# Where TensorE's operands start in SBUF, modulo 256 bytes, and when the loop registers are set

## What is computed

```python
h = layernorm(x) * (1 + ca) + sa
xn = rms_scale * h / (norm(h) + EPS) * split_scale
K = sigmoid(xn @ W_K);  u, g_in, g_out = split(xn @ W_ugg, 3)     # 256 -> 512, 256 -> 3*512
u = u * sigmoid(g_in) * (1 - K)
y = scan(K shifted by one token, u) * sigmoid(g_out) @ W_out + h  # 512 -> 256
x = x + ga * y
h = layernorm(x) * (1 + cb) + sb
for e in range(8):                                               # the two best experts of a token count
    out += (gelu(h @ W1[e] + b1[e]) @ W2[e] + b2[e]) * weight[:, e]
x = x + gb * out
```

## Time and profile before

| | |
|---|---|
| median of three runs | 726.5 us |
| the profiled execution: time, span | 730.45 us, 728.5 us |
| PE busy, weight loads busy | 684.8 us, 625.1 us |
| DVE, ACT, POOL busy | 505.1, 417.0, 399.3 us |
| granted clock of TensorE, mean | 0.984 |
| matmuls L1107 and L1123 (experts), L998 (mixing) | 1536 and 1632, 768 |

### The profile page before, as it was taken

The page is one execution under the profiler, slowest core; times in us unless marked ns, Lnnn a source line. Parts: engine busy times, 40 slices in busy tenths (PEclk is TensorE's granted clock), DMA queues, the critical chain, the costliest instruction groups (busy, mean ns, idle before and its releaser), DMA issues.

```text
span 728.5 us, 16045 instructions
## 1 busy us (share of the span) xinstructions
PE 684.8 (94%) x4798; PEld 625.1 (86%) x4798; DVE 505.1 (69%) x1751; ACT 417.0 (57%) x1068; POOL 399.3 (55%) x318
## 2 busy tenths in 40 slices
PE   5799999999999998998989899999999999999992
PEld 2578878788888887898879899999999999999992
DVE  5869789998988796575754556558775575576451
ACT  4555655556565553664455656647666566566460
POOL 2165536796767567256653437337656356374443
PEclk9899999999999999899999999999999999999997
DMA  8370011302202323245544454567664655544433
GB/s 299 114 242 30 29 59 54 109 30 89 75 16 90 144 75 111 31 117 149 103 82 65 80 119 69 118 143 177 134 124 74 161 99 125 133 70 69 68 74 43
DMA packets 50603, 72.77 MB, mean 100 GB/s; under 512 B 5968, under 2 KB 42396, under 8 KB 50528
## 3 DMA queue, kind: packets, MB, share of 16 engines
q0 software_dynamic: 16480, 27.28, 21.4%
q1 hardware_dynamic: 34048, 44.60, 19.8%
HBM read 48.85 MB, written 23.01 MB: 99 GB/s over the span
## 4 chain that ended last, share of the span: by engine, by line
PE 82%; DVE 6%; issue 4%; DMA 3%; ACT 2%; POOL 1%; another core or an unknown queue 1%; SPq 0%; DVEq 0%; POOLq 0%; ACTq 0%
PE yb L1123 24%; PE mm L998 22%; PE mm L1107 19%; PE yb L1023 7%; PE tp L1098 2%; PE tp L1107 2%; PE yb L1107 2%; DMA gbr<-mod_rows,xm 1%; PE tp L1013 1%; DVE ysb L1583 1%; DVE hl L1554 1%; PE tp L1034 1%; DMA h2all<-in_L_wmod 1%; DVE ytmp L1575 1%
## 5 line engine op out<-in xcount | busy, mean ns | idle before, releaser
L668 POOL DMA_INDIRECT out_x<-ysb,tokb x68 | 110.6, 1627 | 177.7 <-DVE ysb L1583 133.5
L924 ACT ACTIVATE hh<-mm,vT 128x256 fp32r<-128x256 f32 (+1 forms) x232 | 109.6, 473 | 148.5 <-PE mm L1107 130.8
L1123 PE MATMUL yb<-SH,hh 128*128 128x256 f32 x544 | 158.0, 290 | 3.7 <-DVE hl L1554 2.5
L1123 PE MATMUL yb<-SH,hl 128*128 128x256 f32 x544 | 153.3, 282 | 1.2 <-issue 1.0
L1123 PE MATMUL yb<-SL,hh 128*128 128x256 f32 x544 | 153.3, 282 | 1.1 <-issue 1.1
L1554 DVE TENSOR_TENSOR hl<-mm,hh 128x256 fp32r<-128x256 f32 (+1 forms) x232 | 93.4, 407 | 85.3 <-ACT mm L925 69.3
L1107 PE MATMUL mm<-fh,SH 128*128 128x256 f32 x416 | 119.5, 287 | 7.0 <-DVE hl L1554 3.7
L1107 PE MATMUL mm<-fl,SH 128*128 128x256 f32 x416 | 116.8, 281 | 0.0
L1107 PE MATMUL mm<-fh,SL 128*128 128x256 f32 x416 | 116.8, 281 | 0.0
L998 PE MATMUL mm<-xh,WH 128*128 128x512 f32 x256 | 108.1, 422 | 1.8 <-DVE xl L1311 1.8
L1123 PEld LDWEIGHTS yb<-SH,hh 128*128 128x128 f32 x544 | 103.8, 191 | 5.0 <-DVE hl L1554 3.8
(11 more groups left out here) (263 smaller groups left out, 1413.5 us busy)
## 6 DMA issues: line engine op xcount, KB each, us to landing
xin<-disp_x SPq DMA_DIRECT2D x74, 132.0 KB
wraw<-in_L_ffn_W SPq DMA_DIRECT2D x8, 1024.0 KB
h2all<-in_L_ffn_W SPq DMA_DIRECT2D x8, 1024.0 KB
xb<-in_L_attn_x SPq DMA_DIRECT2D x8, 512.0 KB, 7.3
out_x<-x2b SPq DMA_DIRECT2D x8, 512.0 KB
mb<-mod_rows SPq DMA_DIRECT2D x3, 768.0 KB, 6.4
wraw<-in_L_attn_W_ugg SPq DMA_DIRECT2D x1, 1536.0 KB, 11.5
gbr<-mod_rows,xm POOLq DMA_INDIRECT x74
```

The lines of the kernel that those rows point to most:

```text
L668: e.indirect_dma_start(out=out_rows, out_offset=bass.IndirectOffsetOnAxis(ap=tokb[:, j:j + 1], axis=0), in_=ysb[:, j, :], in_offset=None, ...
L924: e.activation(hh[:, f, c_], u, ACT.Gelu_apprx_tanh, bias=bias)
L1123: i = e.matmul(yb[0][:, j * D:(j + 1) * D], a[:, f, j * 128:(j + 1) * 128], b[:, f, :], start=(f == 0 and j == 0 and t == 0), stop=(f == N ...
```

## The change

All of it is about where things lie and when registers are set; no instruction of TensorE, ACT or POOL computes something else.

- **Gaps.** `gap0` (192 bytes) comes before xh0, `gap1` (128 bytes) before fh, `gap2` (64 bytes) before SH1. SH and SL grow by 256 bytes.
- **The second half of SH and SL** starts 192 bytes later (`W2_AT`), so that it lies at 0 modulo 256 when the tensor starts at 64. `split_at` gives the place to write to.
- **One wait** is added on DVE in the last group: the four `split_low(e, 0, q)` also wait for `hx_ready`, since SL0 now reaches into xb0.
- **Registers.** `tile_begins` runs before each early tile on PE, ACT and DVE. Before the eighth (`i == 7`) it sets the registers, each to what the count will be at the end of that tile; then the wait for `counts_ready` and `counts_of` follow. `loops_begin`, where `to_registers` was, issues nothing.

Start addresses modulo 256, worked out from the declarations (loaded, streamed):

| | before | after |
|---|---|---|
| mixing, even g (WH/WL, xh0/xl0) | 128, 64 | 0, 0 |
| mixing, odd g (WH/WL, xh1/xl1) | 128, 128 | 0, 0 |
| project, fp32 (og, wog0 or wog1) | 128, 64 or 128 | 0, 64 or 0 |
| layer1, even expert (SH0/SL0, fh/fl) | 64, 128 | 64, 0 |
| layer1, odd expert (SH1/SL1, fh/fl) | 128, 128 | 64, 0 |
| layer2, even expert (hh/hl, SH0/SL0) | 128, 64 | 64, 0 |
| layer2, odd expert (hh/hl, SH1/SL1) | 128, 128 | 64, 0 |
| half tiles, fp32 (wraw, fr) | 128, 128 | 128, 64 |

All slices taken of these tensors step by multiples of 256 bytes.

```diff
+LINE = 16
+W2_AT = 2048 + 3 * LINE
...
+            sb(gone, "gap0", [128, 3 * LINE])
             xh[0] = sb(gone, "xh0", [128, 2, T], F32R)
...
-        SH[0] = sb(ctx, "SH0", [128, 4096], F32R)
-        SL[0] = sb(ctx, "SL0", [128, 4096], F32R)
+        SH[0] = sb(ctx, "SH0", [128, 4096 + 4 * LINE], F32R)
+        SL[0] = sb(ctx, "SL0", [128, 4096 + 4 * LINE], F32R)
         xin = sb(ctx, "xin", [128, 2, DW])
+        sb(ctx, "gap1", [128, 2 * LINE])
         fh = sb(ctx, "fh", [128, 2, TE], F32R)
...
+        sb(ctx, "gap2", [128, LINE])
+        SH[1] = sb(ctx, "SH1", [128, 4096 + 4 * LINE], F32R)
+        SL[1] = sb(ctx, "SL1", [128, 4096 + 4 * LINE], F32R)
...
+        def split_at(q):
+            c0 = q * 512 if q < 4 else W2_AT + (q - 4) * 512
+            return slice(c0, c0 + 512)
...
+            def tile_begins(i):
+                if i == NE - 2:
+                    then.update(now)
+                if i == NE - 1:
+                    for name in names:
+                        n = 2 * now[name] - then[name]
+                        r = e.alloc_register(f"{engine}_{name}")
+                        e.reg_mov(r, n)
+                        ahead[name] = (r, n)
+            def loops_begin():
+                for name in names:
+                    r, n = ahead[name]
+                    assert n == now[name]
+                    rl[name] = r
...
             for i in range(NE):
+                tile_begins(i)
+                if i == NE - 1:
+                    e.wait_ge(S["counts_ready"], 2)
+                    ks = counts_of(e)
...
-            e.wait_ge(S["counts_ready"], 2)
-            ks = counts_of(e)
-            to_registers()
+            loops_begin()
...
                     e.wait_ge(S["x2_ready"], NG - 2)
+                    e.wait_ge(S["hx_ready"], NG - 1)
                     for q in range(4):
                         split_low(e, 0, q)
```

More of the change, by code:

```diff
@@ L264, in early @@
             return 0 if i < NE0 else 1
+        def split_at(q):
+            c0 = q * 512 if q < 4 else W2_AT + (q - 4) * 512
+            return slice(c0, c0 + 512)
         def split_high(e, n, q):
             r = slice(q * 512, (q + 1) * 512)
+            to = SH[n % 2][:, split_at(q)]
             if q in (0, 4):
@@ L272, in split_high @@
             if q < 4 and n >= 2:
-                e.tensor_copy(SH[n % 2][:, r], wraw[n % 2][:, r]).then_inc(done, 1)
+                e.tensor_copy(to, wraw[n % 2][:, r]).then_inc(done, 1)
             else:
-                e.activation(SH[n % 2][:, r], wraw[n % 2][:, r], ACT.Copy).then_inc(done, 1)
+                e.activation(to, wraw[n % 2][:, r], ACT.Copy).then_inc(done, 1)
         def split_low(e, n, q):
@@ L280, in split_low @@
             e.wait_ge(S["split_high1" if q < 4 else "split_high2"], 4 * n + q % 4 + 1)
-            e.tensor_tensor(SL[n % 2][:, r], wraw[n % 2][:, r], SH[n % 2][:, r].bitcast(F32), ALU.subtract)\
+            e.tensor_tensor(SL[n % 2][:, split_at(q)], wraw[n % 2][:, r], SH[n % 2][:, split_at(q)].bitcast(F32), ALU.subtract)\
                 .then_inc(S["split_low1" if q < 4 else "split_low2"], 1)
@@ L318, in counter @@
             now = dict.fromkeys(names, 0)
-            rl = {}
+            then, ahead, rl = {}, {}, {}
             def grow(name, by):
@@ L341, in to_registers @@
                     rl[name] = r
-            return due, grow, to_registers
+            def tile_begins(i):
[12 more added lines that the diff above has]
+                    rl[name] = r
+            return due, grow, to_registers, tile_begins, loops_begin
         def pads_put(e, n):
@@ L415, in sp_program @@
             r_late = [e.alloc_register("sp_late0"), e.alloc_register("sp_late1")]
-            due, grow, to_registers = counter(e, "sp", ("rows_turned", "meta_copied"))
+            due, grow, to_registers, _, _ = counter(e, "sp", ("rows_turned", "meta_copied"))
             def rows_at(n):
@@ L656, in pool_program @@
             send(g - 2, 1)
-            due, grow, to_registers = counter(e, "pool", ("y_ready", "meta_copied", "y_sent0", "y_sent1", "gb_loaded"))
+            due, grow, to_registers, _, _ = counter(e, "pool", ("y_ready", "meta_copied", "y_sent0", "y_sent1", "gb_loaded"))
             def gather():
@@ L736, in act_program @@
         def act_program(e):
-            due, grow, to_registers = counter(e, "act", ("layer1_done", "layer2_done", "rows_turned", "rows_low"))
+            due, grow, _, tile_begins, loops_begin = counter(e, "act", ("layer1_done", "layer2_done", "rows_turned", "rows_low"))
             def weights_high(part, k):
@@ L980, in pe_program @@
         def pe_program(e):
-            due, grow, to_registers = counter(e, "pe", ("hidden_low", "y_taken", "rows_loaded", "rows_low", "rows_raw"))
+            due, grow, _, tile_begins, loops_begin = counter(e, "pe", ("hidden_low", "y_taken", "rows_loaded", "rows_low", "rows_raw"))
             def main_part(g, hc, part):
@@ L1117, in layer2 @@
             def layer2(n, f, parts, late=False):
-                w2h, w2l = (t[n % 2][:, 2048:4096].rearrange("p (c n) -> p c n", c=NF) for t in (SH, SL))
+                w2h, w2l = (t[n % 2][:, W2_AT:W2_AT + 2048].rearrange("p (c n) -> p c n", c=NF) for t in (SH, SL))
                 if f >= 4 or late:
@@ L1248, in dve_program @@
         def dve_program(e):
-            due, grow, to_registers = counter(e, "dve", ("gelu_done", "rows_high", "layer2_done", "y_taken", "y_sent0", "y_sent1",
+            due, grow, _, tile_begins, loops_begin = counter(e, "dve", ("gelu_done", "rows_high", "layer2_done", "y_taken", "y_sent0", "y_sent1",
                                                          "rows_loaded", "gb_loaded", "dve_d"))
```

2 lines of the change are left out of this document (removed).

## The result

The changed kernel takes 724.1 us, median of 20 runs (720.4 to 728.1); the kernel before, run beside it, 728.5 (725.2 to 731.3). The ratio is 0.9928, 95% interval 0.9914 to 0.9943: faster by 0.7%, some 5 us, where 11 us were forecast. The gain lies near 4 to 5 us.

A forecast was written before the change was run, and what follows sets the result against it. PE's matmuls times their address-dependent pitch were taken to bound the kernel. Experts' addresses 9.5, mixing 1.3 and registers 0.2 us gave 11.0 off the median 726.5: 715.5 us, range 705 to 727.

The forecast's parts named there:

- The bound and the finding: Whole kernel: nearly all time is matmuls times pitch, and pitch depends on start addresses, 113.3 against 120.0 ns in experts.
- Part 1: Experts' matmuls, all at load 64 and stream 0 after the change: pitch 113.3 to 113.7 ns, 9.5 us saved in sum.
- the three terms: Savings behind 375 us: odd tiles 7.8 us, even tiles 1.6, the four half tiles' fp32rs 0.3.
- half way: Rival in the experts: load 64 past stream settles now in the good, now in the slower state; mean 115.8, 721.5 us; chance 0.20.
- The bound of 108 ns: Best possible expert pitch, taken from `project` at 216 ns for 2 x 256 columns.
- The early tiles: Early tiles to the eighth's transposes: 0.6 us from pitch, 1.2 from the odd tile, less a 0.9 us wait; 0.9 saved.
- What a faster PE loses to the gather: Behind half tiles, where DVE waits for the gather of gbr: PE's savings there are lost, 0.8 us in all.
- Part 2: Mixing with load and stream both at 0: even groups fall from 24.20 to 23.85 us, odd ones stay; 1.3 us saved.
- Part 3: Register setting: 1.1 us gone at the loops' start, 0.9 us new wait in the eighth early tile; net 0.2 us.
- A rule of the Trainium skill: PE matmuls: separate read ports, so pitch would not know addresses and only Part 3's gain would come, 726.3 us.
- 2 us were carried each way: Whole forecast: allowance for a 4 us stall and a half-speed clock stretch that may differ between executions.

The follow-up runs named there:

- same_start: Changed kernel with the experts' streamed operands moved from 0 to 64 modulo 256, where the loaded ones lie; 734.05 us, ratio 1.0042 to the kernel before.
- the shifts: shifted_64, shifted_128 and shifted_192: changed kernel with everything put 64, 128 or 192 bytes further, distances kept; ratios to the kernel before 0.9903, 0.9908, 0.9936.
- the pairs' run: Reference left out; TensorE alone at all 16 load and stream start pairs, 256 and 512 columns; same place 120.0 and 226.7 ns, 64 past 113.3 or 117.8 and 233.3.
- changed_again: The changed kernel unaltered, measured once more against the kernel before at 731.25 us; 726.77 us, ratio 0.995.
- registers_late: Changed kernel with VectorE's register moves and count loads put behind the sixth and seventh block of the eighth early tile; 709.11 us against 715.11 before, ratio 0.9913.
- shifted_192: Changed kernel with everything put 192 bytes further, experts loading at 0 and streaming from 192; 710.59 us, ratio 0.9936 to the kernel before.
- addresses_alone: Changed kernel with the register edit taken back and all addresses kept; 727.05 us against 729.71 for the kernel before, ratio 0.995.
- registers_alone: Kernel before with registers set ahead of the eighth early tile and every address as before; 729.51 us, ratio 0.999 to the kernel before.
- shifted_64: Changed kernel with one 64-byte gap ahead of all tensors TensorE reads, experts loading at 128 and streaming at 64; 723.93 us against 729.71 before, ratio 0.9903.
- shifted_128: Changed kernel with everything put 128 bytes further, experts loading at 192 and streaming from 128; 708.85 us against 715.11 for the kernel before, ratio 0.9908.
- shifted_128_late: Changed kernel with everything 128 bytes further and VectorE's register work behind blocks six and seven of the eighth early tile; 723.53 us, ratio 0.9899 to the kernel before.

## Why the prediction was right or wrong

- **The bound and the finding: right.** PE's pitch bounds the kernel and hangs on addresses. same_start, the shifts and the pairs' run show it with nothing else changed. That it is a clash of the two reads is argued; the runs show that the distance of their starts decides, not by what mechanism.
- **Part 1, the pitch of load 64 and stream 0: wrong, and this is the step that failed.** I took 113.3 to 113.7 "by its nearest row", layer2 of an even expert, and explained that row's own last twelve at 118.3 ns away by the change of pairs before them. That was the second pitch of this very distance. The means were 115.2 to 115.5 ns. Summed over all matmuls near that pitch behind 375 us, what lay above 113.3 was 10.5 us before and is 4.9 after: 5.6 us saved where the three terms came to 9.7. These 4.1 us are nearly all of the 4.5 by which the table falls short. The rival "half way" had the mechanism, both its states and a mean of 115.8, at 0.20, and its 5.0 us less is what came (4.4 by the medians, 5.2 by the ratio); the mechanism should have been the forecast, since the only row of that distance held both pitches. The bound of 108 ns reads `project`'s 216 ns as two passes of 256 columns; its row shows the 216 ns, and no run shows the passes.
- **The early tiles: wrong in sign.** +0.9 was forecast and -0.4 came. Both profiles have the clock at half speed in the first early tile; the profile after has it there twice more, for some 3 us each, where before ran at full clock:

```profile
291.50:296.00 4.50, 4.50 (x25) 4.50 (x25) 2.72 (x18) 3.73 (x13) 0.00 (x0) 0.55 0.00 0
336.50:340.50 4.00, 3.56 (x19) 3.56 (x20) 3.36 (x20) 3.91 (x10) 1.79 (x2) 0.58 0.24 58
374.00:378.00 4.00, 4.00 (x21) 4.00 (x22) 2.50 (x8) 1.68 (x5) 2.12 (x2) 0.57 0.28 69
```

  The last two follow waits of PE of 2.1 and 1.4 us. 6.8 us at half clock are 3.4 us of lost work at most, more than the 1.3 us that are missing. In the profiled execution of changed_again the same stretch lasts 97.5 us, 1.6 less than before, and the clock's mean varies between executions of either kernel by some 0.01; so this is a matter of the single execution, for which 2 us were carried each way.
- **What a faster PE loses to the gather: not settled.** 0.8 us was put down. In the profile after it is hardly to be seen (1.4 us of waits for hl in the loops, 1.3 before), and same_start at 119.9 ns has 0.2. With a mean pitch of 114.1 to 115.1 ns three of the shifted kernels have 3.9 to 4.3 us; but at 115.1 to 115.7 ns it is 1.1 in changed_again, 3.1 in registers_late, 5.0 in shifted_192 and 5.3 in addresses_alone. So it varies by 4 us at nearly one pitch. Had the forecast pitch come, some 3 us more might have gone there (an estimate from those three).
- **Part 2, the mixing: right.** 1.15 us by the first cut and 1.4 by the start of group 7 (248.1 before, 246.7 after), 1.3 forecast; even groups fell from 24.20 to 23.73, odd ones from 23.85 to 23.70, a little below the "good" pair.
- **Part 3, the registers: right.** A wait of 0.9 us in the eighth tile as forecast, and 1.6 us less in the first half tile where 1.1 was forecast for the registers: registers_alone has nearly all of it, 9.20 to 7.65, with the eighth tile 1.0 us longer. Nothing can be measured in the whole.
- **A rule of the Trainium skill.** Two runs that differ in addresses alone have tiles of 11.95 us against 11.34 and 11.74. The Trainium skill, TensorE: Matmul & The Clock Gate, Part 2, step 1, has loading take no read bandwidth from the running matmul. The pitch that the prediction derived from it, one that knows no addresses, is not what was measured. Whether the load takes bandwidth or holds the stream up in another way no run tells. The N/2.4 + 2.5 ns that the Trainium skill has for an isolated stream, on the same page under Back-to-back issue gap, was not met either: in no run did a settled stretch go under 113.3 and 226.7 ns, where it has 109.2 and 215.8.

## What to carry to other kernels

When one address pattern shows two pitches within a trace, forecast the mixture, and look in the chain for where one goes over into the other. For 256 streamed columns of this type place the loaded operand 64 bytes past the stream modulo 256, for 512 at the same place, and try the whole layout shifted by 64 bytes at a time; it costs one line of code. Two shifted layouts were some 0.4% under the unshifted one on the same chip, shifted_64 under addresses_alone (with intervals that touch) and shifted_128 with the late registers under the change; shifted_192 was no gain (0.9936). Work moved off one wait goes where its engine has time behind the critical block, not ahead of it.

## What the runs showed of the hardware that was not expected

- The same matmuls on the same addresses hold one of two pitches, 113.3 or 117.8 ns at 256 columns, mostly for a whole tile, and which of them hangs on what stood before. At load 64 and stream 0 alone they repeat a sequence of five rounds, two of them slow; at three other places of the same distance a fast round was followed by a fast one. In shifted_128 a single gap of 160 ns between two matmuls, in place of 113.3, was followed by the slow pitch for the rest of the kernel.
- The order of the distances turns round with the length: same place 120.0 ns at 256 columns (the worst) and 226.7 at 512 (the best); 64 past 113.3 or 117.8 against 233.3 (the worst).
- One of the chips takes 715 us for the kernel before where the others take 728.5 to 731. On it the seven early tiles of shifted_128 last 88.0 us, against 99.4 for the same addresses in shifted_128_late on another chip, and PE's waits there that the profile lays to nothing ("issue") are 0.5 us in 282:375 against 6.2. Its clock also does not fall there, where that of shifted_128_late falls to half for 3.4 us at 337 and at 374.5. What the slower chips wait for was not looked into.
